# The four taps of a causal convolution: from VectorE multiply-adds to accumulating TensorE matmuls, in layer 0 of a two-layer kernel

## What is computed

```python
xn = rmsnorm(x, rms_w)
xz = xn @ in_proj                       # 128 -> 512
xi, z = jnp.split(xz, 2, axis=-1)       # 256 each
xc = conv_general_dilated(xi, conv_w, padding=[(3, 0)], feature_group_count=256) + conv_b   # 4 taps, causal, per channel
xi = silu(xc)
dt, Bm, Cm = split(xi @ x_proj); delta = softplus(dt @ dt_w + dt_b)
# scan over the tokens: h = exp(delta*A) * h + delta*xi*B ;  y = h . C
y = (y + xi * D) * silu(z);  out = x + y @ out_proj
```

## Time and profile before

| | us |
|---|---|
| median of 3 runs (2262.88 to 2268.63) | 2266.21 |
| the profiled execution | 2265.14 |
| its span | 2263.3 |
| of it the prologue, to the first `up` (TensorE) | 94.5 |
| the 15 tiles with a front, to `gt` of the last (TensorE) | 94.5 to 1401 |
| one such tile, mean of ten | 87.4 |
| layer 1 | from 1486 |

### The profile page before, as it was taken

How to read it: one execution, slowest core, us unless ns; L and a number is a source line. 1 busy time by engine, 2 the same in 40 slices (tenths; PEclk the granted TensorE clock), 3 DMA queues, 4 the chain that set the end, 5 groups by cost and what they waited for, 6 DMA issues and landing times. The chain is left out here.

```text
span 2263.3 us, 40460 instructions
## 1 busy us (share of the span) xinstructions
PE 1996.5 (88%) x13648; PEld 1155.7 (51%) x13714; DVE 1732.8 (77%) x2781; ACT 1335.6 (59%) x2421; POOL 1288.6 (57%) x972
## 2 busy tenths in 40 slices
PE   1799999999999999999999999945899999998885
PEld 0455555555555555555555555533455555544442
DVE  3498888888888889888888888854777777765544
ACT  1576776776776776766767767611355555544442
POOL 0477867767767767767768777623322222224540
PEclk9999999999999999999999999955899999998987
DMA  7514505415325335335145055041222222233437
GB/s 192 136 41 107 130 27 127 112 39 128 97 51 132 86 67 132 76 77 132 53 99 131 30 118 122 15 123 63 83 92 87 88 88 88 88 112 102 141 94 227
DMA packets 197004, 222.49 MB, mean 98 GB/s; under 512 B 28872, under 2 KB 139504, under 8 KB 192688
## 3 DMA queue, kind: packets, MB, share of 16 engines
q1 hardware_dynamic: 194736, 215.52, 37.0%
q0 software_dynamic: 2048, 4.18, 0.7%
HBM read 165.41 MB, written 54.27 MB: 97 GB/s over the span
## 5 line engine op out<-in xcount | busy, mean ns | idle before, releaser
L685 POOL TENSOR_TENSOR dBx<-REP,BC 128x1024 f32<-128x1024 f32 x256 | 603.0, 2358 | 288.2 <-DVE dA L845 243.2
L845 DVE TENSOR_TENSOR_SCAN dA<-dA,dBx 128x512 f32<-128x512 f32 x512 | 626.6, 1224 | 115.1 <-ACT dA L555 66.2
L374 PE MATMUL UP<-xnT,W 128*128 128x512 f32 x1024 | 518.4, 626 | 52.0 <-ACT hT L564 40.1
L383 PEld LDWEIGHTS DN<-W,hT 128*128 128x128 f32 x4096 | 469.4, 192 | 109.3 <-issue 97.6
L383 PE MATMUL DN<-W,hT 128*128 128x128 f32 x4096 | 496.0, 278 | 0.3 <-ACT GD L571 0.3
L564 ACT ACTIVATE hT<-UP,b 128x512 f32<-128x512 f32 x512 | 355.1, 694 | 88.7 <-PE UP L374 85.0
L555 ACT ACTIVATE dA<-REP,A 128x512 f32<-128x512 f32 x512 | 354.1, 695 | 72.4 <-DVE PR L854 72.1
L854 DVE TENSOR_TENSOR PR<-dA,BC 128x512 f32<-128x512 f32 x512 | 353.6, 691 | 31.5 <-DVE dA L845 18.8
L1705 DVE TENSOR_REDUCE NM<-S 128x4 f32<-128x1024 f32 (+1 forms) x192 | 234.5, 1221 | 148.5 <-PE S L1264 93.5
L374 PEld LDWEIGHTS UP<-xnT,W 128*128 128x128 f32 x1024 | 180.6, 195 | 278.5 <-issue 146.2
L1466 ACT ACTIVATE PT<-S 128x1024 f32<-128x1024 f32 x192 | 196.4, 1023 | 181.5 <-PE S L1278 135.2
(11 more groups left out here) (246 smaller groups left out, 2809.6 us busy)
## 6 DMA issues: line engine op xcount, KB each, us to landing
REP<-s_delta SPq DMA_DIRECT2D x128, 256.0 KB, 7.8
REP<-s_dx SPq DMA_DIRECT2D x128, 256.0 KB, 7.3
BC<-s_b SPq DMA_DIRECT2D x128, 256.0 KB, 8.7
s_parts<-SPL SPq DMA_DIRECT2D x32, 384.0 KB, 2.8
s_dx<-tz SPq DMA_DIRECT2D x16, 512.0 KB, 3.1
s_y<-zeros SPq DMA_DIRECT2D x32, 256.0 KB, 4.8
WE<-in_L_ffn_we SPq DMA_DIRECT2D x32, 256.0 KB, 4.5
YC<-s_y SPq DMA_DIRECT2D x16, 512.0 KB, 4.9
```

Source lines behind the costliest of these rows:

```text
L374: nc.tensor.matmul(UP[k % 2][:], W1[:, e % E0, f * P:(f + 1) * P], xnT[:, q, :], start=True, stop=True).then_inc(upf.sem, 1)
L383: last = nc.tensor.matmul(DN[:, j * P:(j + 1) * P], hT[:, e % 2, f, j * P:(j + 1) * P], W2[:, e, f, :], start=(f == 0), stop=(f == FB - 1))
L685: nc.gpsimd.tensor_tensor(dBx[:, s % 2], DX[:, h, j:j + 2, :], BC[:, q // 2, q % 2, :].unsqueeze(1).to_broadcast([P, 2, T0]), ALU.mult).th ...
L845: nc.vector.tensor_tensor_scan(h, h, dBx[:, k // 2 % 2, k % 2, :], 0.0, ALU.mult, ALU.add).then_inc(scan_done.sem, 1)
```

## The change

In-projection and taps are both linear, so channel c of tap s is a matmul of the shifted input with in_proj's columns scaled by w[c, 3-s]. Four weight tiles `taps[:, k, :]` (128x256 each) are made once, from in_proj, the rms weight and conv_w, which is now loaded broadcast to all partitions (512 KB in place of 4 KB). Each of `x0` and `x1` becomes four matmuls that add up in FRO, the later three on outputs and inputs shifted by s tokens. ScalarE's `tap` scales by 0.5 alone and adds the bias. VectorE's six multiply-adds per tile and the semaphore conv_step go; who waited for it waits for ScalarE's tap_done. Some steps of the front stand elsewhere in the tables.

```diff
-    convw = sb("convw", [P, HALF, 4]); ...
+    convw = sb("convw", [P, HALF * P, 4]); taps = sb("taps", [P, 4, HALF * P]); ...
-        (convw[:], dram["L0_attn_conv_w"].rearrange("(h p) k -> p h k", p=P)),
+        (convw[:], dram["L0_attn_conv_w"].rearrange("(a c) k -> a c k", a=1).to_broadcast([P, HALF * P, 4])),
-    PE_AT = dict(xqt=-2, x0=0, x1=4, out=8, xproj=10, dt0=12, dt1=16, xnt=17, logits=19, z0=24, z1=27, gt=30)
-    ACT_AT = dict(xr=-2, tap0=2, tap1=4, tanh=6, ..., tz0=24, tz1=27, gt=29)
-    DVE_AT = dict(conv0=3, conv1=4, xi=8, soft=19, lg=19, lnw=20, gate1=22, z0=25, gate2=26, z1=28, ev1=3, store=9, stat=13, ev0=21)
-    POOL_AT = dict(..., ff=10, r=20, dx=22, rank=24, yz1=3, yz0=22, delta=20, lg=21, keep=27)
+    PE_AT = dict(xqt=-1, x0=0, x1=4, out=8, xproj=10, dt0=12, dt1=16, xnt=17, logits=18, z0=24, z1=26, gt=29)
+    ACT_AT = dict(xr=-2, tap0=2, tap1=4, tanh=6, ..., tz0=24, tz1=26, gt=28)
+    DVE_AT = dict(xi=8, soft=19, lg=20, lnw=20, gate1=22, z0=25, gate2=26, z1=28, ev1=1, store=9, stat=14, ev0=21)
+    POOL_AT = dict(..., ff=13, r=20, dx=22, rank=24, yz1=0, yz0=22, delta=20, lg=21, keep=26)
-    SP_AT = dict(bst=12, dst=15, est=24, bc0=28, save=8, load=12)
+    SP_AT = dict(bst=12, dst=15, est=25, bc0=27, save=8, load=12)
...
+            for k in range(HALF):
+                if h == PE_AT[f"x{k}"]:
+                    if k == 0:
+                        pe.wait_ge(xT_copied.sem, xT_copied.at(n, 1))
+                    else:
+                        pe.wait_ge(tap_done.sem, tap_done.at(n, 1))
+                    cols = slice(k * P, (k + 1) * P)
+                    nc.tensor.matmul(FRO[:], taps[:, 3, cols], xrT[:], start=True, stop=False)
+                    for s in range(1, 4):
+                        last = nc.tensor.matmul(seqs(FRO[:])[:, :, s:], taps[:, 3 - s, cols], seqs(xrT[:])[:, :, :L - s], start=False, stop=(s == 3))
+                    last.then_inc(front.sem, 1)
...
-                    nc.scalar.activation(xch[:, k, :], FRO[:], ACT.Identity, scale=convw[:, k, 3:4], bias=convb[:, k:k + 1]).then_inc(tap_done.sem, 1)
+                    nc.scalar.activation(xch[:, k, :], FRO[:], ACT.Identity, scale=0.5, bias=convb[:, k:k + 1]).then_inc(tap_done.sem, 1)
...
-        nc.vector.tensor_scalar(inproj[:], inproj[:], rmsw[:], None, ALU.mult)
-        nc.vector.tensor_scalar(convw[:], convw[:], 0.5, None, ALU.mult)
+        for k in range(4):
+            nc.vector.scalar_tensor_tensor(taps[:, k, :], inproj[:, 0:HALF * P], rmsw[:], convw[:, :, k], ALU.mult, ALU.mult)
+        nc.vector.tensor_scalar(inproj[:, HALF * P:], inproj[:, HALF * P:], rmsw[:], None, ALU.mult)
...
-            for b in range(HALF):
-                if h == DVE_AT[f"conv{b}"]:
-                    dve.wait_ge(tap_done.sem, tap_done.at(n, 1 + b))
-                    src, dst = seqs(FRO[:]), seqs(xch[:, b, :])
-                    for k in range(1, 4):
-                        if k > 1:
-                            dve.wait_ge(conv_step.sem, conv_step.at(n, 3 * b + k - 1))
-                        nc.vector.scalar_tensor_tensor(dst[:, :, k:], src[:, :, :L - k], convw[:, b, 3 - k:4 - k], dst[:, :, k:],
-                                                       ALU.mult, ALU.add).then_inc(conv_step.sem, 1)
```

More of the change, by code:

```diff
@@ L79, in layer0 @@
     inproj = sb("inproj", [P, 4 * P]); rmsw = sb("rmsw", [P, 1])
-    convw = sb("convw", [P, HALF, 4]); convb = sb("convb", [P, HALF])
+    convw = sb("convw", [P, HALF * P, 4]); taps = sb("taps", [P, 4, HALF * P]); convb = sb("convb", [P, HALF])
     xproj = sb("xproj", [P, HALF, 2 * S + RANK]); dtw = sb("dtw", [P, HALF * P]); dtb = sb("dtb", [P, HALF])
@@ L119, in layer0 @@
     sp_done = signal("sp_done", 3); relu_done = signal("relu_done", E0 * FB); da_ready = signal("da_ready", TILES); gated = signal("gated", E0)
-    conv_step = signal("conv_step", 6); gate_step = signal("gate_step", 9); lg_done = signal("lg_done", 1); gate_made = signal("gate_made", 5); z_done = signal("z_done", 2); xi_done = signal("xi_done", 1)
+    gate_step = signal("gate_step", 9); lg_done = signal("lg_done", 1); gate_made = signal("gate_made", 5); z_done = signal("z_done", 2); xi_done = signal("xi_done", 1)
     log_step = signal("log_step", 2); delta_done = signal("delta_done", 1)
@@ L192, in layer0 @@
     EARLY = 7
-    PE_AT = dict(xqt=-2, x0=0, x1=4, out=8, xproj=10, dt0=12, dt1=16, xnt=17, logits=19, z0=24, z1=27, gt=30)
-    ACT_AT = dict(xr=-2, tap0=2, tap1=4, tanh=6, dtb=10, d0=14, d1=16, xn=18, exp=17, one=17, ln=18, gexp=20, tz0=24, tz1=27, gt=29)
-    DVE_AT = dict(conv0=3, conv1=4, xi=8, soft=19, lg=19, lnw=20, gate1=22, z0=25, gate2=26, z1=28, ev1=3, store=9, stat=13, ev0=21)
-    POOL_AT = dict(xm=-7, xq=-4, xs=-4, ff=10, r=20, dx=22, rank=24, yz1=3, yz0=22, delta=20, lg=21, keep=27)
+    PE_AT = dict(xqt=-1, x0=0, x1=4, out=8, xproj=10, dt0=12, dt1=16, xnt=17, logits=18, z0=24, z1=26, gt=29)
+    ACT_AT = dict(xr=-2, tap0=2, tap1=4, tanh=6, dtb=10, d0=14, d1=16, xn=18, exp=17, one=17, ln=18, gexp=20, tz0=24, tz1=26, gt=28)
+    DVE_AT = dict(xi=8, soft=19, lg=20, lnw=20, gate1=22, z0=25, gate2=26, z1=28, ev1=1, store=9, stat=14, ev0=21)
+    POOL_AT = dict(xm=-7, xq=-4, xs=-4, ff=13, r=20, dx=22, rank=24, yz1=0, yz0=22, delta=20, lg=21, keep=26)
     GATE_AT = 3
     ACC_AT = 2
-    SP_AT = dict(bst=12, dst=15, est=24, bc0=28, save=8, load=12)
+    SP_AT = dict(bst=12, dst=15, est=25, bc0=27, save=8, load=12)
     def place(k):
@@ L433, in slot @@
                 else:
-                    output(it - 1, 1 - par, lambda: pe.wait_ge(conv_step.sem, conv_step.at(it + 1, 6)))
+                    output(it - 1, 1 - par, lambda: pe.wait_ge(tap_done.sem, tap_done.at(it + 1, 2)))
         def fore(h, n, q):
@@ L443, in fore @@
                 last.then_inc(front.sem, 1)
[L444 to L451, removed]
+            for k in range(HALF):
[9 more added lines that the diff above has]
+                    last.then_inc(front.sem, 1)
             if h == PE_AT["xproj"]:
                 pe.wait_ge(xi_done.sem, xi_done.at(n, 1))
-                pe.wait_ge(conv_step.sem, conv_step.at(n, 6))
+                pe.wait_ge(tap_done.sem, tap_done.at(n, 2))
                 pe.wait_ge(x_done.sem, x_done.at(n - 2, 1))
@@ L610, in fore @@
                     act.wait_ge(front.sem, front.at(n, 2 + k))
-                    nc.scalar.activation(xch[:, k, :], FRO[:], ACT.Identity, scale=convw[:, k, 3:4], bias=convb[:, k:k + 1]).then_inc(tap_done.sem, 1)
+                    nc.scalar.activation(xch[:, k, :], FRO[:], ACT.Identity, scale=0.5, bias=convb[:, k:k + 1]).then_inc(tap_done.sem, 1)
             if h == ACT_AT["tanh"]:
-                act.wait_ge(conv_step.sem, conv_step.at(n, 6))
+                act.wait_ge(tap_done.sem, tap_done.at(n, 2))
                 act.wait_ge(delta_done.sem, delta_done.at(n - 1, 1))
@@ L790, in _ @@
     def _(dve):
-        for s in (conv_step, gate_step, z_done, xi_done, log_step, scan_done, prod_done, ev_done, x_done, restat):
+        for s in (gate_step, z_done, xi_done, log_step, scan_done, prod_done, ev_done, x_done, restat):
             dve.sem_inc(s.sem, 2 * s.per)
```

## The result

| | before | after |
|---|---|---|
| median of 4 runs (us) | 2265.87 (2262.88 to 2268.63) | 2320.91 (2318.1 to 2322.73) |
| the profiled execution | 2265.14 | 2318.1 |
| its span | 2263.3 | 2316.3 |

The changed kernel takes 1.0235 times as long (95% interval 1.0218 to 1.0253): 2.3% slower. The forecast was 2319.0, between 2298 and 2338.

The account below looks back on a forecast made before the run. TensorE was taken to bound layer 0, VectorE following with slack. +3.26 us per tile, +48.9 for 15 tiles, plus 4 for the prologue, on 2265.14 gave 2318.0, stated as a 2319 us median; range 2298 to 2338.

Parts of the forecast that it names:

- six matmuls: At x0 and x1 on TensorE, three more matmuls each at 0.86 us per 512 columns: +5.12 us per tile.
- x1's wait for conv0: TensorE's wait at x1 for VectorE's convolution, 13.0 us over 15 tiles, goes: 0.87 us less per tile.
- gt and xqt apart: Gate transpose and xqt no longer stand back to back, with `down` between them: 0.59 us less per tile.
- the softplus stage: With logits earlier, one long TensorE wait becomes two short ones; length unchanged, but 0.4 of 0.75 us clock cost saved per tile.
- the branch: TensorE's wait at the loop's branch, 9.4 us in all before, was listed but given no term in the sum.
- prologue: Before the loop, six more matmuls cost 5.1 to 10.3 us, two convolutions save 4.7: +0.4 to +5.6, taken as +4.
- The first rival: TensorE has room, new matmuls cost under 0.31 us each and VectorE's relief counts: faster, down to 2238 us; chance 7%.
- The next three cover nothing: At x0 and x1, one matmul already covers the 0.57 us wait for relu, so the three added ones hide none.
- the xrT copy: ScalarE's copy waits for the later xqt, with x0 two `up` (1.8 us) later as cover: costed at nothing.
- the third rival: The 2.60 us relu wait shrinks by half, returning 1.3 us in 15 tiles, 20 us in all: 2299 us; chance 9%.
- a sign of being wrong: The forecast would be wrong if, among other signs, the softplus stretch became shorter.
- The second rival: At h = 0 to 4, VectorE waits at ev1, x1 then waits 1 to 2 us per tile: 2334 to 2349 us; chance 12%.

Follow-up runs that it names:

- e8: Kernel before, convolution still on VectorE, with the front's new places except xqt, ev1, yz1, conv0 and conv1: 2264.83 us, ratio 0.9928 to before.
- e3: Kernel before without VectorE's six multiply-adds per tile (three older taps left out): 2250.82 us, ratio 0.9916 to before.
- e2: Changed kernel with the newest tap alone, x0 and x1 one matmul each: 2232.22 us, ratio 0.9842 to the kernel before.
- e6: Changed kernel with 32 small matmuls put ahead of the loop, shifting its body: 2321.13 us, ratio 1.0169 to the kernel before.
- e5: Kernel before with x0 and x1 each cut into four matmuls of 128 columns: 2295.3 us, ratio 1.0059 to before.
- e12: Changed kernel unaltered, measured again in the session of the last experiments: 2335.92 us, ratio 1.0237 to the kernel before.

## Why the prediction was right, term by term

| term | predicted | measured |
|---|---|---|
| six matmuls, per tile | +5.12 | +5.1 (0.85 each, start to start) |
| x1's wait for conv0, per tile | -0.87 | -1.17 (9 x 1.75 and 5 x 0.1, over 14) |
| gt and xqt apart, per tile | -0.59 | -0.77 (30.88 - 29.09 - 2.56; e8 alone gives 28.33 - 29.09 = -0.76) |
| the softplus stage, per tile | -0.40 | -0.58 (mean of 14) |
| the branch, per tile | 0 | +1.06 (5 x 2.97 / 14) |
| sum per tile, 14 tiles | +3.26 | +3.66 |
| prologue | +4 | -2.6 |
| first tile | +3.26 | +1.7 |
| last tile, layer 1 | 0 | +2.6 |

**Who is the bound: right.** TensorE set the pace. Taking 71.5 us from VectorE gave 18 (e3), and giving TensorE six matmuls per tile cost 89 (e2). The first rival needed new matmuls under 0.31 us; they are 0.85. The Trainium skill ("Perfetto Trace Analysis", Identifying the Most-Contended Engine) judges TensorE's headroom by two measures, the FLOP utilization and the weight loads' busy share. By the second, the one that the first rival used, there should be room: it is 51.88 of 91.1 us per tile, 57%. The distances between starts and e2 show none, so that measure misleads here.

**The price of a matmul: right.** 0.86 was taken from another row of the same shape; the accumulating, shifted ones have it too. "The next three cover nothing" holds against e8 (2.55 for three) and fails against e2, where they cover 0.9 us. What was wrong is the cost of nothing for the xrT copy behind the later xqt, with two `up` as its cover. With x0 as one matmul it costs 0.93 (29.26 in e2, 28.33 in e8); its real cover is the work that the same change adds to x0. For the gT copy, nothing was right in the tiles (e8). In the last tile, where x0 is missing, an `up` waits for a relu twice, which with the dearer pairs behind is 1.1 of its 1.8 us:

```profile
1455.88 2.31 PE L374 MATMUL UP<-xnT,W 128*128 128x512 f32 x4 [0.61 <-ACT hT L568]
...
1465.30 2.31 PE L374 MATMUL UP<-xnT,W 128*128 128x512 f32 x4 [0.62 <-ACT hT L568]
```

The first of these stands in e8's last tile too (0.61), so xqt and ev1 do not make it; the second does not. What makes each was not tested by itself.

**x1's wait and gt/xqt: right in kind, too small.** I took idle time from the list of waits. A wait also spoils what is behind it: the matmul after it starts some tenths later than it could, and after a long one the next pair is slow. The distance between the marks counts that, the list of waits does not.

**The softplus stage: right.** The wait splits as described (0.99 at logits, 1.34 at `up`, predicted 1.1 and 1.5):

```profile
1059.83 1.06 PE L483 MATMUL FRO<-Wr,xnT 128*128 128x8 f32 x8 [0.99 <-ACT xnT L638]
...
1065.83 2.31 PE L374 MATMUL UP<-xnT,W 128*128 128x512 f32 x4 [1.34 <-ACT hT L568]
```

The shortest softplus stage is 11.68 before and 11.68 after, as it should be if ScalarE's burst sets it, and with VectorE relieved alone (e3) the stage is no shorter, so the third rival has nothing. By the mean the stage did become shorter (12.39 to 11.81), which I had named as a sign of being wrong although my own sum booked 0.40 there; only a lower floor would have been such a sign. Above that floor stands the clock. Two stretches of the changed kernel, the same place of two tiles (length, busy by engine, granted clock, DMA):

```profile
1057.00:1064.50 7.50, 6.50 (x45) 5.00 (x43) 6.56 (x9) 7.41 (x10) 4.72 (x3) 1.00 0.00 0
1155.00:1162.50 7.50, 7.34 (x30) 5.22 (x30) 7.27 (x10) 7.32 (x13) 5.10 (x5) 0.77 0.00 0
```

At 1.00 the `down` behind logits starts 1.87 us ahead of its `up`; at 0.77 it takes 3.28. Before, 10 of 15 pairs behind the long wait were slow; now none is, but the `down` behind logits is slow in about half of the tiles. I took 0.4 of at most 0.75; it gave 0.58.

**The second rival: its premise came, its consequence did not.** VectorE waits at ev1 for a YS that comes later, up to 8.3 us in tiles with a branch:

```profile
DVE y L865 <- PE YS L395: 48.5, 15, 8.3
```

But no x1 waits. VectorE is busy 72.0 per tile (said 71.7) and idle 19.1 (said 19); "most of it before y" was wrong, since y is 3.2 of it.

**The branch: the step that failed.** I listed "9.4 at the loop's branch" as a wait of before and let it stand unchanged, without a line in the sum or in the range. A change that adds instructions inside a loop can change what its jump costs. It grew by 2.97 us in the first stage, 5 x 2.97 = 14.9 us, more than a quarter of the whole loss: in part a longer wait, in part matmuls behind it at the lower clock. That tiles with a branch grew by 4.86 more than the others, and not by 2.97, has another reason, which the sum did not miss: x1's wait had stood almost only in tiles without a branch, and I had booked its end as a mean over all.

**The prologue: wrong in sign.** I weighed +0.4 to +5.6 and took +4. TensorE in order of time there, after:

```profile
39.87 4.57 PE L454 MATMUL FRO<-xrT,taps 128*128 128x510 f32 x6
45.28 1.12 PE L452 MATMUL FRO<-xrT,taps 128*128 128x512 f32 x2 [0.84 <-ACT xch L615]
...
52.08 1.91 PE L462 MATMUL FRO<-xi,xproj 128*40 128x512 f32 x4 [3.12 <-DVE xi L914]
```

The -2.6 has three parts. x0 starts 1.45 us later (38.01, before 36.56), since the first tile's input comes later; I had put nothing, at most 3. From x0 to xproj it takes 14.07 us instead of 13.70 (xproj began at 50.26), the low end of my range: x0's new matmuls start at the slow price, as the row says, x1's run at the fast one, and the convolutions' 4.7 pay for them. From xproj to gt it takes 37.88 instead of 42.29, and these 4.4 us I had not counted: xproj's row is 1.91 instead of 3.64, the first dt's 1.12 instead of 2.07, logits' 1.06 instead of 1.88. I had looked for denser matmuls to get faster only among the new ones, not behind them.

So 2319 was hit because errors cancelled. The sum lacked 14.9 us at the branches and 2.6 at the end. Against that stand 9.2 us by which the savings in 14 tiles were larger than I gave, 1.6 in the first tile and 6.6 in the prologue. Without the branch's growth the median would have been about 2306, inside the range, but 13 us from the number. The mechanisms in the tiles, the direction and the bound were right; the fit to 2 us was luck.

## What to carry to other kernels

Move work to an engine only if the list of waits and the starts show that it has room; the busy shares alone, that of its weight loads above all, did not tell. When a change adds instructions in a loop, put a line for the backward branch into the sum, and try a written-out loop or a shifted body before judging the change. Compare distances between fixed marks, tiles with and without a branch apart: a wait that goes may have been paying for another.

## What the runs showed of the hardware

- The wait of TensorE at a backward branch depends on where the loop's body lies (e6) and grew when the body got longer (e5, where length and place cannot be told apart): 1.7 to 2.1 us before, 3.3 to 4.1 after, at most 3.5 with 12 more matmuls and no more columns in the body (e5), at most 2.5 with the changed body shifted by 32 small matmuls (e6). Over all kernels with the loop, those with 126 packets on the instruction queue had 13.4 to 18.7 us for five branches, those with 120 or 121 had 8.7 to 10.7.
- The branch costs more than its wait: behind 3.53 us of idleness the next three f32 matmuls of 512 columns took 5.3 us instead of 2.7, at a granted clock of 0.50.
- A matmul that adds to a PSUM bank through views of two shifted pieces (2x255, 2x254, 2x253) costs what a plain one of 512 columns does, 0.85 us.
- In the prologue the page's granted clock does not tell what the matmuls do. The stretch from 35 to 60 us reads 1.00 before, though x0 and x1 take 2.07 there; after, it reads 0.94, with x1 at 1.12. I leave this open.
- The same two kernels were 0.7% longer in other sessions, with their ratio unchanged (e12); the difference lies in layer 1, not in the tiles.
